# The last norm's sum in PSUM: where a feed-forward keeps the small values of its normalization

## What is computed

```
xn       = layernorm(x) * g + b
abel     = gelu(xn @ aw1 + ab1) @ aw2 + ab2                    # 512 hidden
nonabel  = rotate(mixture(xn))                                 # six experts of 256 hidden, the best two weighted
gate     = sigmoid([abel, nonabel] @ gc_w + gc_b)
out      = layernorm(x + (x + abel * (1 - gate) + nonabel * gate))
```

## Time and profile before

| | |
|---|---|
| median of three runs | 697.62 us (696.67 to 697.83) |
| the profiled execution's own time | 695.79 us |
| its span, first to last instruction | 694.1 us |
| mean granted TensorE clock | 0.976 of full speed |
| busy over the span: PE | 644.0 us, 93% |
| DVE | 495.8 us, 71% |
| ACT | 449.0 us, 65% |
| POOL | 502.0 us, 72% |

### The profile page before, as it was taken

One profiled execution on the slowest core, in us unless ns is written; L12 is line 12 of the kernel. 1 busy time (PEld: TensorE's weight loads), 2 busy tenths in 40 slices (PEclk: granted clock), 3 DMA queues, 4 the chain that ended last, 5 costly groups with the idle time before them and its releaser, 6 DMA issues. The chain is left out here.

```text
span 694.1 us, 10135 instructions
## 1 busy us (share of the span) xinstructions
PE 644.0 (93%) x3215; PEld 491.7 (71%) x3215; DVE 495.8 (71%) x1047; ACT 449.0 (65%) x626; POOL 502.0 (72%) x290
## 2 busy tenths in 40 slices
PE   5979999999999999999999999999797899989883
PEld 4657778777777777777877777776586687667651
DVE  3578668678777866866977887681297878776684
ACT  3547667676776676766767767676456477657561
POOL 8028888898888988888888888899753356567660
PEclk9999999999999999999999999999988899999996
DMA  7532222312222221322132222207000000000001
GB/s 196 137 76 62 47 46 62 77 45 47 47 69 69 47 47 46 83 55 46 46 68 68 47 47 47 47 0 196 3 2 1 0 2 1 1 16 0 15 1 31
DMA packets 29076, 33.75 MB, mean 49 GB/s; under 512 B 6977, under 2 KB 15970, under 8 KB 28898
## 3 DMA queue, kind: packets, MB, share of 16 engines
q1 hardware_dynamic: 29026, 33.14, 19.9%
HBM read 6.84 MB, written 1.05 MB: 11 GB/s over the span
## 5 line engine op out<-in xcount | busy, mean ns | idle before, releaser
L357 POOL TENSOR_TENSOR probs_l<-probs,probs_h 128x1024 fp32r<-128x1024 f32 (+1 forms) x160 | 347.4, 2185 | 96.2 <-ACT probs_h L399 50.5
L454 DVE TENSOR_REDUCE m_part<-max_ps 128x1 f32<-128x512 f32 (+2 forms) x320 | 180.0, 602 | 84.2 <-PE max_ps L529 63.4
L396 ACT ACTIVATE probs<-scores 128x1024 f32<-128x1024 f32 (+1 forms) x160 | 150.5, 941 | 125.8 <-PE scores L558 67.1
L590 PE MATMUL out_ps<-probs_h,v 128*128 128x512 f32 (+5 forms) x640 | 186.1, 374 | 2.1 <-POOL probs_l L357 2.1
L399 ACT ACTIVATE probs_h<-scores 128x1024 fp32r<-128x1024 f32 (+1 forms) x160 | 149.7, 936 | 0.0
L859 POOL TENSOR_TENSOR hid_lo<-hid,hid_hi 128x512 fp32r<-128x512 f32 x64 | 84.0, 1317 | 53.8 <-ACT hid_hi L939 41.4
L557 PE MATMUL scores<-q,k 128*128 128x512 f32 (+1 forms) x320 | 122.0, 382 | 0.0
L590 PE MATMUL out_ps<-probs_l,v 128*128 128x512 f32 (+1 forms) x320 | 116.4, 364 | 0.0
L558 PE MATMUL scores<-q,k 128*128 128x512 f32 (+1 forms) x320 | 116.3, 364 | 0.0
L590 PEld LDWEIGHTS out_ps<-probs_h,v 128*128 128x128 f32 (+1 forms) x640 | 95.7, 163 | 23.9 <-POOL probs_l L357 5.8
L529 PE MATMUL max_ps<-k,q 128*128 128x512 f32 (+2 forms) x320 | 101.8, 393 | 5.6 <-DVE m_part L454 5.2
(11 more groups left out here) (195 smaller groups left out, 977.3 us busy)
## 6 DMA issues: line engine op xcount, KB each, us to landing
k<-qk SPq DMA_DIRECT2D x96, 128.0 KB, 2.3
q<-qk SPq DMA_DIRECT2D x96, 128.0 KB, 2.3
q<-m_turn SPq DMA_DIRECT2D x128, 0.5 KB
v_all<-L_ffn_ew SPq DMA_DIRECT2D x2, 768.0 KB, 7.9
probs<-L_attn_x SPq DMA_DIRECT2D x4, 256.0 KB, 4.3
pos<-positions SPq DMA_DIRECT2D x1, 1024.0 KB, 6.6
out<-v_all SPq DMA_DIRECT2D x4, 256.0 KB, 2.3
acc<-L_attn_Wqkv SPq DMA_DIRECT2D x6, 128.0 KB, 2.9
```

What stands on the lines that cost most here:

```text
L357: pool.tensor_tensor(probs_l[:, p % 2, :, lo:CH], probs[:, p % 2, :, lo:CH], probs_h[:, n % 3, :, lo:CH], ALU.subtract).then_inc(S["probs_ ...
L396: act.activation(probs[:, p % 2, :, lo:CH], scores[:, p % 2, :, lo:CH], ACT.Exp, scale=D ** -0.5).then_inc(S["probs_ready"], 1)
L454: dve.tensor_reduce(m_part[:, r, j:j + 1], max_ps[:, u % 2, 0:width], AX.X, ALU.max).then_inc(S["tile_max_ready"], 1)
L590: last = pe.matmul(o_ps(h, c)[0:rows, lo:CH], v, pr, start=(p == PAIR0[c] and j == 0 and k == 0), stop=(p == PAIR0[c + 1] - 1 and j == 1 a ...
```

## The change

The last norm's sum is written over the turned mixture in bank 6 in place of its own tile in SBUF, and the statistics and the scales read it there. Of the small values, `var`, `half`, `t` and `bits` lie in the first 16 columns of bank 7, the gate's bank, and `guess` alone stays in SBUF; that holds for the norms of sections 2, 3 and the last. In section 1 bank 7 is in use for the features and weights of the second half, so there (`second`) all five stay in SBUF, as they do for the norms ahead of the feed-forward. A Newton round forms var x guess and then -0.5 times that times guess, where it formed guess x guess and then -0.5 times var times that; so each of its instructions reads `guess` and one other value. And as bank 6 is read until the norm's end, PE's rotation at `T_ROTATE` waits for the whole norm of the chunk before, where it waited for its sum.

```diff
--- before.py
+++ after.py
@@ -621,8 +621,7 @@
 def layer_norm(dve, sem, base, src, dst, buf, n):
 
 
-    stats, mean_var, s, pause = buf
-    var, half, guess, t, bits = (s[:, i, 0:n] for i in range(5))
+    stats, mean_var, (var, half, guess, t, bits), pause = buf
     if not isinstance(base, int) or base > 0:
         dve.wait_ge(sem, base)
     for i in range(n):
@@ -649,10 +648,10 @@
     yield
     for k in range(3):
         dve.wait_ge(sem, base + 3 + 3 * k)
-        dve.tensor_tensor(t, guess, guess, ALU.mult).then_inc(sem, 1)
+        dve.tensor_tensor(t, var, guess, ALU.mult).then_inc(sem, 1)
         yield
         dve.wait_ge(sem, base + 4 + 3 * k)
-        dve.scalar_tensor_tensor(half, var, -0.5, t, ALU.mult, ALU.mult).then_inc(sem, 1)
+        dve.scalar_tensor_tensor(half, t, -0.5, guess, ALU.mult, ALU.mult).then_inc(sem, 1)
         yield
         dve.wait_ge(sem, base + 5 + 3 * k)
         dve.scalar_tensor_tensor(guess, half, 1.5, guess, ALU.add, ALU.mult).then_inc(sem, 1)
@@ -718,8 +717,8 @@
         gw, gb, gcb = early.gw, early.gb, early.gcb
         y1 = sb("y1", [P, NT, E])
         u = sb("u", [P, NT, E])
-        ln_buf = (sb("ln_stats", [P, NT // 2, 6])[:], sb("ln_mean_var", [P, NT // 2, 2])[:], sb("ln_small", [P, 5, NT // 2])[:],
-                  sb("ln_pause", [P, 1])[:])
+        ln_stats, ln_mean_var = sb("ln_stats", [P, NT // 2, 6])[:], sb("ln_mean_var", [P, NT // 2, 2])[:]
+        ln_small, ln_pause = sb("ln_small", [P, 5, NT // 2]), sb("ln_pause", [P, 1])[:]
         xn = sb("xn", [P, T])
         xn_hi = sb("xn_hi", [P, T], F32R)
         xn_lo = sb("xn_lo", [P, T], F32R)
@@ -767,9 +766,17 @@
         nonabel = sb("nonabel", [P, CH])
         delta = sb("delta", [P, CH])
         mixed = sb("mixed", [P, CH])
-        last_sum = sb("last_sum", [P, TPC, E])
 
         ps = ctx.enter_context(nc.psum_tensor("ps_ffn", [P, 8, CH], F32))
+
+        ln_buf = (ln_stats, ln_mean_var, [ln_small[:, i, :] for i in range(5)], ln_pause)
+
+        def last_sums(second):
+
+            if second:
+                return (*ln_buf[0:2], [ln_small[:, i, 0:TPC] for i in range(5)], ln_pause)
+            var, half, t, bits = (ps[:, 7, i * TPC:(i + 1) * TPC] for i in range(4))
+            return ln_stats, ln_mean_var, (var, half, ln_small[:, 0, 0:TPC], t, bits), ln_pause
 
         names = """loaded_eb2 eb2_cleared pick_made before_made identities_made weights_cleared attention_turned
             generator_turned generator_squared series_multiplied exponential_squared exponential_turned
@@ -1156,10 +1163,10 @@
                         dve.wait_ge(S["mixed_turned"], c)
                         ts = bass.ds((c - 1) * TPC, TPC)
                         wait(dve, S["last_norm_steps"], ln_steps(TPC) * (c - 1))
-                        dve.scalar_tensor_tensor(last_sum[:], y1[:, ts, :], 2.0, ps[:, 6, :].rearrange("p (t e) -> p t e", e=E),
-                                                 ALU.mult, ALU.add).then_inc(S["second_residual_ready"], 1)
+                        last_sum = ps[:, 6, :].rearrange("p (t e) -> p t e", e=E)
+                        dve.scalar_tensor_tensor(last_sum, y1[:, ts, :], 2.0, last_sum, ALU.mult, ALU.add).then_inc(S["second_residual_ready"], 1)
                         dve.wait_ge(S["second_residual_ready"], c)
-                        norm = layer_norm(dve, S["last_norm_steps"], ln_steps(TPC) * (c - 1), last_sum[:], y2[:, ts, :], ln_buf, TPC)
+                        norm = layer_norm(dve, S["last_norm_steps"], ln_steps(TPC) * (c - 1), last_sum, y2[:, ts, :], last_sums(second), TPC)
                     if prev and j >= T_NORM:
                         for _ in range(NORM_STEPS[j - T_NORM]):
                             next(norm)
@@ -1340,7 +1347,7 @@
                     if prev and j == T_ROTATE:
                         pe.wait_ge(S["rotation_low_ready"], 1)
                         pe.wait_ge(S["moe_low_ready"], c)
-                        wait(pe, S["second_residual_ready"], c - 1)
+                        wait(pe, S["last_norm_steps"], ln_steps(TPC) * (c - 1))
                         for k, (a, m) in enumerate(((rot_hi, moe_hi), (rot_lo, moe_hi), (rot_hi, moe_lo))):
                             last = pe.matmul(ps[:, 6, :], a[:], m[:], start=(k == 0), stop=(k == 2))
                         last.then_inc(S["moe_rotated"], 1)
```

## The result

| | before | changed |
|---|---|---|
| median | 697.73 us (696.67 to 698.72, six runs) | 693.0 us (691.76 to 694.4, six runs) |
| ratio | | 0.9938, 95% interval 0.9919 to 0.9957 |
| profiled execution | 695.79 us, span 694.1 | 694.4 us, span 692.7 |

The changed kernel is faster by 4.7 us, 0.62%. A second series of nine runs gave 693.01 us and a ratio of 0.9941 (0.9921 to 0.9961). The profiled execution of the changed kernel is the slowest of its six, so the two spans side by side (694.1 and 692.7) say too little; the stretches have to be compared one by one.

A forecast was written before the change was run, and what follows sets the result against it. TensorE was taken to set the feed-forward's pace, stalled by DVE norm steps held by POOL. Section 2 -2.6, section 3 -1.4, section 1 +0.15, last section +0.25: -3.6 us, from 697.62 to 694.0 us, range 692.3 to 696.2.

The forecast's parts named there:

- What bounds, and what a hold is: Feed-forward: TensorE sets the pace; an all-SBUF DVE step started while POOL works is held until POOL is done.
- Section 2, -2.6 us: End of section 2: without holds the next section's PE work starts earlier; gain 2.6 us, between 2.2 and 2.8.
- Section 3, -1.4 us: End of section 3: POOL finishes block 15 at 674.1 and PE starts then in place of 675.51; gain 1.4 us.
- The price of PSUM: DVE's norm: +0.013 us for the sum, 0.1 for eight small writes, 0.15 (0 to 0.27) for four scales.
- scales of over 0.4 us each: The norm's four scales: over 0.4 us each was named as a sign that the prediction is wrong.
- The small steps: Norm's twelve steps on small values: eight write PSUM, at +0.013 us each, 0.1 us for eight.
- the last norm: Last section, where DVE alone sets the end: 0.013 us for the sum, 0.1 small writes, 0.15 scales; +0.25.
- The waits: PE's rotation waits for the whole previous norm but reaches that step later than the norm's end; nothing is late.
- The clock: Clock fell to half after PE's 1.4 us stop before L1345; with less idling it may not fall.
- Section 1's slower scales: End of section 1: four scales on the way to the next chunk's `hid_hi`, +0.15 us (0 to 0.27).
- the rival that I gave 12%: Last section: the clock stays up at the rotation, 1.2 to 1.3 us more reach the end, 692.7 us; 12%.
- The likeliest case in its pure form: Whole kernel: gains in sections 2 and 3 less PSUM costs, -3.6 us, 694.0 us; 693.2 to 695.0 had 64%.

The follow-up runs named there:

- variance only: The changed kernel with only `var` of the small values in bank 7, half, guess, t and bits in SBUF, the sum in bank 6; ratio to before 0.9984.
- POOL short: The kernel before, all in SBUF, with POOL subtracting only 64 of 512 columns of `hid_lo`, the rest zero; 683.28 us in one run.
- section 1's sum in SBUF: The changed kernel with the sum of section 1 in a tile in SBUF, later sections as in the change; 692.15 us, ratio to before 0.9925.
- the sum alone: The changed kernel with all small values in SBUF in every section, only the sum in bank 6; 700.35 us, ratio to before 1.0033.
- the Newton round alone: The kernel before with only the new Newton round and PE's rotation waiting for the whole previous norm, all in SBUF; 697.81 us, ratio 1.0005.
- small values alone: The changed kernel with the sum in a tile in SBUF again, small values still in bank 7; 692.76 us, ratio to before 0.9923.
- section 1 too: The changed kernel with the small values of section 1 in bank 7 as well; 689.69 us, ratio to before 0.9880.
- the same with the last section in SBUF: The changed kernel with small values in bank 7 in section 1 as well, but sum and small values in SBUF in the last section; 687.79 us, ratio 0.9870.

## Why the prediction was right

The forecast was 694.0 us in 692.3 to 696.2, and 693.0 came. Step by step:

*What bounds, and what a hold is*: right. An all-SBUF step that starts beside POOL lasts until POOL's instruction is done. Three runs show it from three sides: PSUM operands free the step (the change), the hold moves with the operands (variance only), its length is POOL's (POOL short). The Trainium skill, SBUF — State Buffer, section "Who interferes with whom", says that VectorE's second pair of SBUF ports is shared with GpSimd and locked for a whole instruction, and that a DVE instruction with at most one SBUF input outside the double-rate modes is not in it; by that rule the trace agrees in each case: the one-source steps that were held had source and output in SBUF, the two-source ones both inputs.

*Section 2, -2.6 us*: -2.56. *Section 3, -1.4 us*: -1.44. (These are the stretches between rotations. By the sections' own bounds, which the prediction used, section 3 takes 678.45 - 650.21 = 28.24 us, 28.3 foretold, but section 2 takes 650.21 - 620.90 = 29.31 and not 27.7, for the clock's fall at its start lies in it; in the kernel with section 1's sum in SBUF, where the clock stays up, it is 27.76.) Here every term can be found again: the product 0.77 us behind the EPS step (0.8 foretold), POOL's blocks back to back, DVE's `hid_hi` at 648.25 - 643.87 = 4.38 behind the EPS step (644.15 - 639.82 = 4.33 foretold).

*The price of PSUM*: the scales cost (1.36 - 1.12) = 0.24 us for four, by the median 402 ns and not 344 each, near the upper bound of 0.27; I had taken 0.15. The prediction had called scales of over 0.4 us each a sign of being wrong: they lie on that line, and this term was set too low. The small steps: from the EPS step to the scales in the last section

```profile
686.17 0.17 DVE L639 TENSOR_SCALAR ps_ffn<-ln_mean_var 128x4 f32<-128x4 f32 x1
...
688.58 1.36 DVE L661 TENSOR_SCALAR v_all<-ps_ffn,ln_mean_var,ln_small 128x128 f32<-128x128 f32 x4
```

688.58 - 686.17 = 2.41 us for twelve, against 2.38; +0.03 where I had put 0.1. The Trainium skill, VectorE: DVE Perf Modes, section on the TRN2 errata, puts a step from PSUM to SBUF 62 cycles above one from SBUF to SBUF; by that figure these twelve would take 0.8 us more (an estimate from that page), which this row does not bear out. Together the last norm, from the sum's addition to the last scale, is 5.85 us long and was 5.54: +0.31, where +0.25 was foretold.

*The waits*: right. PE's later wait costs nothing (ratio 1.0005, together with the Newton round).

*The clock*: here the sum was incomplete on both sides, and the errors nearly cancel, which is luck. Section 1's slower scales were given 0.15 us; the stretch cost 1.77, since PE's stop grew from 1.57 to 1.81 us and the clock fell behind it. I had asked what the clock would do only at the end, not what 0.25 us more of a stop would do where it was still up. And at the last rotation it stayed up, the rival that I gave 12%, with 1.2 to 1.3 us to gain: -1.44 in the stretch with 0.31 of PSUM's price in it, so some 1.75 by the clock (1.52 against the kernel with section 1's sum in SBUF, whose last norm is the same and whose clock fell: 15.77 - 14.25). The likeliest case in its pure form (clock as before in both places) gives -3.6; the profile gives +1.77 - 2.56 - 1.44 - 1.44 = -3.67, by other terms. The medians say -4.7, with -3.0 to -5.7 by the interval, and -3.67 lies within it. The microsecond between them can lie in the kernel before: its second profile, where the clock fell earlier, has four stretches of 106.68 us together, 5.3 more than the 101.38 of the changed kernel's second, and its execution took 697.13 us, nearer to the median than the first's 695.79. How often before runs with which pattern, no run here shows, and the part of the span ahead of the stretches scatters by one to two microseconds besides.

## What to carry to other kernels

A small step that should take 0.2 us and takes as long as the neighbour engine's instruction is a matter of where its operands lie: with a PSUM operand in every step, even one of four columns, it is free of POOL, at next to no price for small operands and 0.06 us per 128 columns where a double-rate SBUF step is given up. For a one-source step either its source or its output did; in every two-source step here it was one of the two inputs, and whether an output in PSUM alone would do, no run shows. So move to PSUM the steps that run beside POOL, and leave in SBUF those that run alone. And where an edit lengthens a stop of TensorE by a quarter of a microsecond, look at the granted clock behind that stop before pricing the edit.

## What the runs showed of the hardware

Not expected: behind the stop before section 2 the clock fell in all four profiles (of three kernels) whose stop was 1.81 or 1.82 us (the change, twice, the sum alone and the variance alone: 0.57 to 0.59 over the next 4 us) and in none of the six with 1.56 to 1.58 us (before, twice, the Newton round alone, small values alone, section 1's sum in SBUF, twice). A fall there costs some 1.5 us. But the length of the stop alone doesn't decide it: in the kernel with the sum alone PE stops 1.93 us before section 3, and the clock stays at 1.00. Nor is it known why the clock at the last rotation fell in the kernels that had kept it before section 2 with 1.57 us of stop, and stayed up in the three that had removed that stop (section 1 too, the same with the last section in SBUF, and POOL short) and in the change and the variance-only kernel, which had had their fall; the sum alone had both. That stays open: the executions here differ in too much at once to tell.
